# Gate, bias and token order moved to the sorted expert rows; one adding transfer a batch brings them back

## The reference

```
xn = layernorm(x)                                  # 4096 rows of 128
logits = xn @ wr + br;  top_p, top_i = top_k(softmax(logits), 2)
gate = top_p[:, 0] / (top_p[:, 0] + top_p[:, 1])   # one number a row
for e in range(8):                                 # only the rows whose first choice is e count
    hout = gelu(xn @ w1[e] + b1[e]) @ w2[e] + b2[e]
    out += where(top1 == e, hout * gate, 0)
x = x + attention(xn) @ w_proj + b_proj + out
```

## Time and profile before

| | us |
|---|---|
| median of 3 runs | 475.69 |
| the profiled execution, its own time | 475.12 |
| its span, first to last instruction | 473.5 |
| PE busy | 398.5 (84%) |
| DVE busy | 302.1 (64%) |
| ACT busy | 281.0 (59%) |
| POOL busy | 245.2 (52%) |

### The profile page before, as it was taken

The page is one execution under the profiler, slowest core; times in us unless marked ns, Lnnn a source line. Parts: engine busy times, 40 slices in busy tenths (PEclk is TensorE's granted clock), DMA queues, the critical chain, the costliest instruction groups (busy, mean ns, idle before and its releaser), DMA issues. The chain is left out here.

```text
span 473.5 us, 11202 instructions
## 1 busy us (share of the span) xinstructions
PE 398.5 (84%) x3872; PEld 233.1 (49%) x3872; DVE 302.1 (64%) x494; ACT 281.0 (59%) x692; POOL 245.2 (52%) x370
## 2 busy tenths in 40 slices
PE   3736788798989884999999899898899889899884
PEld 2435524343434342999999644344444444444322
DVE  3565389977377765255555477787778678778401
ACT  3521146466376662666666666776667657667762
POOL 6441015358568865122232358778597586653221
PEclk9775559789599997799999999999999999999987
DMA  9999013537237424122222143443354243100000
GB/s 174 259 308 276 24 47 105 154 95 228 77 115 204 130 85 107 45 71 69 66 66 66 35 94 100 142 113 97 93 141 111 81 108 80 41 9 3 24 1 24
DMA packets 45341, 48.14 MB, mean 102 GB/s; under 512 B 7393, under 2 KB 39426, under 8 KB 45170
## 3 DMA queue, kind: packets, MB, share of 16 engines
q1 hardware_dynamic: 41424, 40.41, 30.9%
q0 software_dynamic: 3296, 6.76, 4.7%
q10 hardware_dynamic: 578, 0.40, 0.3%
HBM read 25.39 MB, written 21.89 MB: 100 GB/s over the span
## 5 line engine op out<-in xcount | busy, mean ns | idle before, releaser
L570 ACT ACTIVATE probs<-ps 128x512 f32<-128x512 f32 (+2 forms) x384 | 190.6, 527 | 107.4 <-PE ps L1162 103.8
L723 DVE TENSOR_REDUCE mx<-ps 128x2 f32<-128x1024 f32 (+2 forms) x192 | 196.7, 1045 | 76.3 <-PE ps L1014 70.3
L1162 PE MATMUL ps<-stack 61*128 61x128 bf16 (+3 forms) x512 | 125.0, 313 | 21.7 <-ACT probs L570 20.4
L917 POOL TENSOR_SCALAR_AFFINE_SELECT probs<-probs 128x512 f32<-128x512 f32 x128 | 80.9, 638 | 94.0 <-ACT probs L570 91.9
L1007 PE MATMUL ps<-stack 59*128 59x256 bf16 (+3 forms) x512 | 101.2, 318 | 5.2 <-DVE mx L723 5.1
L1136 PE MATMUL ps<-probs,vt 128*18 128x512 f32 (+3 forms) x1024 | 98.0, 456 | 6.1 <-POOL probs L917 5.7
L1162 PEld LDWEIGHTS ps<-stack 61*128 61x128 bf16 x512 | 35.9, 94 | 123.3 <-ACT probs L570 82.7
L1014 PE MATMUL ps<-tri,swap_b 64*128 64x64 bf16 (+1 forms) x384 | 70.6, 206 | 0.0
L1014 PE MATMUL ps<-tri,cbf 64*128 64x64 bf16 (+1 forms) x384 | 65.2, 205 | 0.0
L899 POOL DMA_DIRECT2D ys_sorted<-yst x39 | 21.1, 540 | 62.2 <-DVE yst L775 61.9
L545 ACT ACTIVATE hid<-ps,wcur 128x128 f32<-128x128 f32 x156 | 44.8, 374 | 0.5 <-PE ps L1094 0.5
(11 more groups left out here) (119 smaller groups left out, 394.8 us busy)
## 6 DMA issues: line engine op xcount, KB each, us to landing
stack<-qk_parts SPq DMA_DIRECT2D x64, 192.0 KB, 4.3
qk_parts<-qkp SPq DMA_DIRECT2D x16, 384.0 KB, 2.6
qk_parts<-qkp SPq DMA_DIRECT2D x16, 256.0 KB, 2.5
wall<-L_ffn_w SPq DMA_DIRECT2D x16, 256.0 KB, 3.0
xs_sorted<-probs SPq DMA_DIRECT2D x1, 2496.0 KB, 11.4
xst<-xs_sorted SPq DMA_DIRECT2D x39, 64.0 KB, 1.8
ys_sorted<-yst POOLq DMA_DIRECT2D x39, 64.0 KB, 2.1
xt<-L_attn_x SPq DMA_DIRECT2D x8, 256.0 KB, 6.9
```

The lines of the kernel that those rows point to most:

```text
L570: act.activation(p[:, e, slots[0]:slots[0] + ns], ps[:, ST_BANK[c % 2], 0:ns * w].rearrange("p (s w) -> p s w", s=ns), ACT.Exp).then_inc(e ...
L723: dve.tensor_reduce(mx[:, n % 2, :, slots[0]:slots[0] + k, tb], src, AX_X, ALU.max, negate=True).then_inc(mx_done, 1)
L917: pool.affine_select(out=p, in_=p, compare_op=ALU.is_ge, fill=0.0, base=0, pattern=[[0, G], [1, P]], channel_multiplier=-1).then_inc(p_mas ...
L1162: last = pe.matmul(ps[:, ST_BANK[c % 2], i * w:(i + 1) * w], stack[at:at + N_STACK, b % 2, 1, 2 * g + s, P * sb_:P * (sb_ + 1)], stack[at: ...
```

## The change

Each normed row gets two more columns (`XW = 130` instead of 128): the gate, written there by DVE (the reciprocal of `route_gate`), and the token's number, written once by POOL at the start with an iota. Padding slots get token numbers past the real ones, by a second iota over the zeroed array. So the scatter to `xs_sorted` and the load of a sorted tile carry gate and token, in rows of 520 bytes where they had 512.

In the expert loop POOL first copies both out of the loaded tile (`tile_meta`, two copies of one column); DVE after its addition does a second operation, yst * gate + b_proj (with b_attn's part in it, `bpb`), and only that sets `ye_done`; POOL stores the tile with an indirect DMA to its tokens' places in `ys_token`. Before it takes the columns of tile n+1, POOL waits for the store of tile n-2; SP's load of a tile waits for `meta_done` beside `xsT_ps`.

After the experts, POOL issues for batch b one DMA at (n, c) = (12 + b, 4) that adds 512 rows to x in SBUF. The gathers, the multiplications by gate, the additions and the bias additions on POOL are gone.

```diff
-        xs_dram = nc.dram_tensor("xs_sorted", (NST * P, C), F32, kind="Internal").ap()
-        ys_dram = nc.dram_tensor("ys_sorted", (NST * P, C), F32, kind="Internal").ap()
+        xs_dram = nc.dram_tensor("xs_sorted", (NST * P, XW), F32, kind="Internal").ap()
+        ys_dram = nc.dram_tensor("ys_token", (NT * P + NST * P, C), F32, kind="Internal").ap()
...
             def load_tile(q, r):
                 if not first(q):
                     sp.wait_ge(xsT_ps, FR * (q - 1) + r + 1)
+                    sp.wait_ge(meta_done, FR * (q - 1) + r + 1)
...
-                dve.reciprocal(gate[:], gexp[:]).then_inc(gate_done, 1)
+                dve.reciprocal(xn[:, :, C], gexp[:]).then_inc(gate_done, 1)
...
                 dve.tensor_tensor(yst[:, r, :], ps[:, r, P:P + C], wcur[:, r, B2_AT:B2_AT + C],
-                                  ALU.add).then_inc(ye_done, 1)
+                                  ALU.add).then_inc(ye_made, 1)
+                dve.wait_ge(meta_done, FR * q + r + 1)
+                dve.wait_ge(ye_made, FR * q + r + 1)
+                dve.scalar_tensor_tensor(yst[:, r, :], yst[:, r, :], gcur[:, r:r + 1], bpb[:], ALU.mult, ALU.add
+                                         ).then_inc(ye_done, 1)
...
             pool.memset(probs[:], 0.0).then_inc(zero_made, 1)
+            pool.wait_ge(zero_made, 1)
+            pool.iota(probs[:, 0:NST * XW].rearrange("p (n w) -> p n w", w=XW)[:, :, C + 1], pattern=[[1, NST]],
+                      base=NT * P, channel_multiplier=NST, allow_small_or_imprecise_dtypes=True).then_inc(zero_made, 1)
+            pool.iota(xn[:, :, C + 1], pattern=[[P, NT]], base=0, channel_multiplier=1,
+                      allow_small_or_imprecise_dtypes=True).then_inc(tokens_made, 1)
...
+            def tile_meta(q, r):
+
+                n = FR * q + r
+                pool.wait_ge(xs_loaded[r], 16 * (q + 1))
+                pool.sem_inc(pool_passed, 1)
+                pool.tensor_copy(gcur[:, r:r + 1], xst[:, r, C:C + 1])
+                pool.tensor_copy(tok[:, r:r + 1], xst[:, r, C + 1:C + 2]).then_inc(meta_done, 1)
+
             def store_tile(q, r):
-                pool.wait_ge(ye_done, FR * q + r + 1)
+                n = FR * q + r
+                if not (final(q) and r == FR - 1):
+                    if not (first(q) and r < FR - 1):
+                        pool.wait_ge(ys_stored[(r + 1) % FR], 16 * (q if r < FR - 1 else q + 1))
+                    tile_meta(q + 1 if r == FR - 1 else q, (r + 1) % FR)
+                pool.wait_ge(meta_done, n + 1)
+                pool.wait_ge(ye_done, n + 1)
                 pool.sem_inc(pool_passed, 1)
-                pool.dma_start(ys_dram[bass.ds((FR * q + r) * P, P), :], yst[:, r, :]).then_inc(ys_stored[r], 16)
+                pool.indirect_dma_start(ys_dram, bass.IndirectOffsetOnAxis(ap=tok[:, r:r + 1], axis=0),
+                                        yst[:, r, :], None).then_inc(ys_stored[r], 16)
...
-                if n % 3 == 1 and c == 6 and n < 3 * NB:
-                    own = xt[:, TB * b:TB * (b + 1), :]
-                    pool.tensor_tensor(own, own, bpb[:].unsqueeze(1).broadcast_to([P, TB, C]), ALU.add
-                                       ).then_inc(biased, 1)
...
-                        pool.indirect_dma_start(ysg[:, d, t, :], None, ys_dram,
-                        pool.tensor_tensor(own, own, gate[:, TB * d:TB * (d + 1)].unsqueeze(2).broadcast_to([P, TB, C]),
...
+                    if (n, c) == (fold_in(d), FOLD_AT):
                         if proj_first(d):
                             pool.wait_ge(proj_added, d + 1)
-                        pool.tensor_tensor(own, own, ysg[:, d], ALU.add).then_inc(ys_added, 1)
+                        pool.dma_start(xt[:, TB * d:TB * (d + 1), :],
+                                       ys_dram[T * d:T * (d + 1), :].rearrange("(n p) c -> p n c", p=P),
+                                       accum_op=ALU.add).then_inc(folded[d], 16)
```

More of the change, by code:

```diff
@@ L26 @@
 NST = NT + E - 1
+XW = C + 2
 EPS = 1e-5
@@ L74, with fold_in @@
 LOADS, STORES = 4, 3
-FETCH_AT = (1, 5)
-def fetch_from(b):
-    return FFN_AT + 2 * b
+FOLD_AT = 4
+def fold_in(b):
+    return FFN_AT + 1 + b
 def proj_at(b):
     return NG * (b + 1) + 1
-def add_at(b):
-    return fetch_from(b) + 2 if proj_at(b) != fetch_from(b) + 2 else fetch_from(b) + 3
 def proj_first(b):
-    return proj_at(b) < add_at(b)
+    return proj_at(b) < fold_in(b)
 def block_kernel(nc, x, w_attn, b_attn, w_proj, b_proj, w1, b1, w2, b2, wr, br,
@@ L127, in block_kernel @@
         guard_p = sb("guard_p", [P, 2, P], BF16)
-        ysg = xn[:].rearrange("p (r n) c -> p r n c", n=TB)
-        xst = sb("xst", [P, FR, C])
+        xst = sb("xst", [P, FR, XW])
+        gcur = sb("gcur", [P, FR])
+        tok = sb("tok", [P, FR], U32)
         xsT = sb("xsT", [P, FR, P])
@@ L285, in block_kernel @@
         proj_added = sem("proj_added")
-        biased = sem("biased")
-        gathered = [sem(f"gathered{r}") for r in range(2)]
-        gated = sem("gated")
-        ys_added = sem("ys_added")
+        meta_done = sem("meta_done")
+        ye_made = sem("ye_made")
+        tokens_made = sem("tokens_made")
+        folded = [sem(f"folded{b}") for b in range(NB)]
         out_stored = [sem(f"out_stored{r}") for r in range(2)]
@@ L477, in normalise @@
                 act.wait_ge(nmr_done, b + 1)
-                act.activation(xn[:, t, :], xt[:, t, :], ACT.Identity, bias=nmr[:, t:t + 1], scale=rstd[:, t:t + 1]
+                act.activation(xn[:, t, 0:C], xt[:, t, :], ACT.Identity, bias=nmr[:, t:t + 1], scale=rstd[:, t:t + 1]
                                ).then_inc(xn_act_done, 1)
@@ L626, in normalise @@
                 for t in range(TB * b, TB * b + 2):
-                    last = dve.tensor_scalar(xn[:, t, :], xt[:, t, :], mv[:, t, 0:1], rstd[:, t:t + 1],
+                    last = dve.tensor_scalar(xn[:, t, 0:C], xt[:, t, :], mv[:, t, 0:1], rstd[:, t:t + 1],
                                              ALU.subtract, ALU.mult)
@@ L785, in experts @@
                 dve.wait_ge(experts_known, 1)
+                dve.wait_ge(bias_made, 1)
                 for r in range(FR):
@@ L925, in pool_at @@
                         pool.wait_ge(slots_done, 1)
+                        pool.wait_ge(gate_done, 1)
+                        pool.wait_ge(tokens_made, 1)
                         pool.wait_ge(zero_stored, 16)
@@ L969, in transposes @@
                 for t in range(TB):
-                    last = pe.transpose(ps[:, XT_BANK[b % 2], t * P:(t + 1) * P], xn[:, TB * b + t, :], ident[:])
+                    last = pe.transpose(ps[:, XT_BANK[b % 2], t * P:(t + 1) * P], xn[:, TB * b + t, 0:C], ident[:])
                 last.then_inc(xnT_ps, 1)
@@ L1084, in tile_transpose @@
                     pe.wait_ge(ye_done, n - FR + 1)
-                pe.transpose(ps[:, r, 0:P], xst[:, r, :], ident[:]).then_inc(xsT_ps, 1)
+                pe.transpose(ps[:, r, 0:P], xst[:, r, 0:C], ident[:]).then_inc(xsT_ps, 1)
             def tile_up(q, r):
```

33 lines of the change are left out of this document (8 added, 25 removed).

## The result

The kernel went from 475.23 us (474.73 to 480.38) to **488.9 us** (488.01 to 489.68, four runs each): ratio 1.025, 95% interval 1.0194 to 1.0306. The forecast was 484.0, its range 470 to 503. A later comparison of the same two kernels on another chip gave 483.55 us beside 478.28 for the kernel before, ratio 1.0073 (1.0033 to 1.0113).

A forecast was written before the change was run, and what follows sets the result against it. PE's own work was taken to bound the loop, with the wait for `ye_done` becoming the pace: 475.1 + 15.4 (loop) + 0.4 + 0.8 - 1.2 - 2.7 - 3.8 (clock) = 484.0 us, range 470 to 503.

The forecast's parts named there:

- the likeliest case: Whole kernel: the forecast itself, 484.0 us, had chance 0.60; as outcomes, slower 0.51, same 0.41, faster 0.08.
- The round over `ye_done`: Expert loop: PE's transpose of n+3 waits for DVE on n; the second operation lengthens this from 1.72 to 2.08 us.
- The collision of 0.2 us a tile: Expert loop: POOL's small copies and DVE's work disturb each other, 0.2 us a tile charged, making the tile 2.28 us.
- It holds by 0.3: Expert loop: SP's load, waiting for `meta_done`, lands in time for the transpose of n+3, with 0.3 us to spare.
- The copy round: Expert loop: the weights' copy after `ye_done` is felt by PE if delayed more than 0.1 us; no separate price.
- POOL sheds work: Outside the loop: less POOL work saves 2.7 us before it (-1 to -3.8) and 1.2 after (0 to -2.5).
- The clock of group 5: Attention, 119 to 134 us: with PE's earlier wait shortened, the half-clock stretch likely does not come, -3.8 us (0 to -4).
- The iotas: Kernel start: two iotas ahead of POOL's first normalisation, 0.2 us each, +0.4 us (0 to 0.4).
- End of the loop: After the last tile: later `ye_done`, an indirect last store and the waits behind it, +0.8 us (0.4 to 2).
- Lock: Rival, expert loop: each wide DVE copy loses 1.14 us beside POOL's indirect DMA; 2.85 us a tile, 505.7 us; chance 0.17.
- PE's pace: Rival, expert loop: the round stays at 1.85 us, below 1.9, so the loop adds 0 to 1; 469.1 us; chance 0.13.
- Rows of 520 bytes: Rival, scatter before the loop: rows cut in two make indirect DMAs a quarter longer; 493.8 us; chance 0.10.

The follow-up runs named there:

- e6: Kernel before plus a second DVE operation of the same shape on `yst` ahead of `ye_done`, POOL's work unchanged: 484.66 us, 2.071 us a tile.
- e1: Changed kernel with PE's transpose waiting for DVE's addition, not its second operation: 478.88 us, ratio 1.0035 to the kernel before, 2.121 us a tile.
- f1: Changed kernel with POOL taking gate and token of tile n+2, not n+1, ahead of the store of n, into six slots: 479.38 us, 2.116 a tile.
- e8: Changed kernel with PE's transpose waiting for DVE's addition and the weights' copy ahead of the second operation: 491.71 us, 2.387 us a tile.
- f4: Changed kernel: columns taken two tiles ahead, transpose and group 11 entry after DVE's addition, POOL's last-store wait before the first adding transfer: 474.40 us, 2.045 a tile.
- f3: As f4, with the weights' copy also ahead of DVE's second operation: 470.66 us, ratio 0.9837 to the kernel before, 1.932 us a tile.
- e3: Changed kernel plus four POOL additions of the removed bias addition's shape, on a spare tile in groups 1, 4, 7 and 10: 486.77 us, ratio 1.0154.
- e5: Changed kernel without DVE's second operation, gate and bias left out; stores, copies and adding transfers stay: 472.51 us, ratio 0.9896 to the kernel before, 1.961 a tile.
- e2: Changed kernel with POOL's wait for the last three stores moved from the loop's end to ahead of the first adding transfer: 481.0 us, ratio 1.0080.

## Why the prediction was right, and where it was not

The time was right (484.0 for 488.9, or 483.55 on the second chip) and the likeliest case was the one that came, but it came near in part by luck, since errors of size offset each other: the loop was put 4.4 us too high, and the clock behind it was left out. On the second chip the cost was 0.7%, where 1.8% was forecast.

**The round over `ye_done`: right.** e6 shows it with nothing else changed: 2.071, where I had 2.08 from dependencies alone. The parts: the second operation 352 ns, not 319; the gap between the two DVE operations 0.04 in e6, as I had, and 0.10 in the kernel after, where DVE waits for `meta_done` as well; release to PE 0.07 in the tile shown and 0.15 at the median, for my 0.14.

**The collision of 0.2 us a tile: failed.** The second operation takes at most 388 ns, 36 over its median, and the wide copy 764 at the median. The loop cost 11.0 us where this term made it 15.4; without it 38 x (2.08 - 1.875) = 7.8. What came on top, from 2.08 to 2.171, is the larger gap, the third round and the one late load. Something does collide, but POOL pays: where its one-column copies overlap the second operation they end 0.03 to 0.04 us behind it and take 0.30 to 0.35 us instead of 0.17 to 0.20 (229.49 in the timeline above). The evidence for a loss on DVE was misread: the row of 3.42 us holds three copies, and they are

```profile
L766 DVE COPY wcur<-wall x1: 762/762/762, 182.7 to 182.7; 128x1156 f32 x1
```

```profile
L766 DVE COPY wcur<-wall x1: 2002/2002/2002, 183.4 to 183.4; 128x1156 f32 x1
```

and a third of 0.75. The first lies beside the indirect DMA (182.46 to 183.54) and lost nothing; the second, which lost 1.24 us, lies beside the two masks (183.56, 1.22 us). No mask runs in the loop.

**"It holds by 0.3": failed.** I had SP's load wait for `meta_done` with 0.3 us to spare. The terms were near and the test was at the wrong place: 2.6 + 1.9 us were set against 3 T - 2.0 at T = 2.28, which had the collision in it. Without the collision, at T = 2.08, the same sum is 0.26 us short, and solved for T it gives (2.6 + 1.9 + 2.0) / 3 = 2.17 us, the step that was measured (so close by luck: the traces make it 2.15). The loads' 3.45 us of room became 0.17, and by e1, f1 and e8 the POOL round binds about as much as the bank. In the kernel after the two share the loss; f1 shows that without this round the loop would still take 2.12. The copy round I had named ("a delay of more than 0.1 us is felt too") and not priced: f4 against f3 prices it at 0.11 (0.185 over tiles 12 to 36), once the two others are gone.

**POOL sheds work: right.** Before the loop I had -2.7 and got -2.1: group 4 -0.8 (0.9), group 7 -1.2 (0.6), the stretch from group 10 to the first addition -0.5 (1.2), group 8 +0.4. After it -1.3 for -1.2: the eight adding transfers take 1.30 us each on POOL, inside the 0.54 to 2.2 allowed.

**The clock of group 5: right**, -3.8 as forecast, and e3 shows the cause: with POOL's additions back, PE's wait for POOL's mask and the fall come back together. The loop kept 1.00, as expected.

**The clock elsewhere: not in the sum.** Group 11 at 0.67 (+2.8) and the last part at 0.50 (+5.3) are 8.1 us that no term held; the second belongs to no part of the change. I had looked at what the change takes away from PE's waits and not at the place where it adds one: PE's wait for `guard_n` behind the loop was 0.44 us and became 1.12, in a stretch in which PE is busy 1.16, 1.08 and 0.66 of 2 us; and its wait for DVE behind the last tile was 0.39 and became 0.84. By e5 and e6 each of the two growths is enough.

**Small terms.** The iotas: POOL's first normalisation starts at 6.72 for 6.58, +0.1 (I had 0.4). The +1.4 up to group 3 is not theirs: e2 and f3 have them too and reach group 3 at 97.2 and 97.5 (97.3 before); in the kernel after the clock had fallen by 27 to 30 us (0.82, where before, e2 and f3 had 1.00). End of the loop +1.1 for +0.8.

**The rivals.** *Lock*: refuted, and the rows of before refuted it already (the copy of 0.76 beside the indirect DMA). In f3 the copy runs wholly beside the store, and neither waits for the other; of its timeline:

```profile
231.88 1.07 POOL L931 DMA_INDIRECT ys_token<-yst,tok  x1 [0.61 <-issue]
...
232.07 0.76 DVE L769 COPY wcur<-wall 128x1156 f32 x1 [0.24 <-DVE yst L778]
...
235.71 0.97 POOL L931 DMA_INDIRECT ys_token<-yst,tok  x1 [0.55 <-issue]
235.80 0.77 DVE L769 COPY wcur<-wall 128x1156 f32 x1 [0.24 <-DVE yst L778]
```

The Trainium skill, SBUF — State Buffer, section "Who interferes with whom", has a DVE copy in a 2-port mode and a GpSimd operation exclude each other for a whole instruction. The copy beside the masks agrees: 0.76 + 1.22 = 1.98 us, measured 2.00. For an indirect DMA it does not hold: the copy keeps 0.76 and the store pays 0.1 us (0.97 or 1.07, by where the copy falls; two of f3's 39 took 1.29 and 1.37), so there the measurement decides. *PE's pace*: refuted by 2.171, yet f3 comes near it (1.932). *Rows of 520 bytes*: refuted, the indirect DMAs of the scatter, L952 in the kernel after, for the gather of the same size before:

```profile
L952 POOL DMA_INDIRECT xs_sorted<-xn,slot x32: 958/980/1234, 102.3 to 177.2; - x32
```

## What to carry to other kernels

An operation added behind a signal lengthens every round that passes through that signal: list who waits for it, and give each waiter the earliest signal that it needs (the bank is free after the read, the weights' copy needs no gate). Rounds of nearly one length hide each other: one broken alone gains a tenth or less of what all give together (0.02 of 0.275 us a tile, tiles 12 to 36), and moving work within one can lengthen another (e8). Test each round's room at the shortest step that the other terms allow, not at one that holds a guess. A wait in a queue says only that something waited; measure the room from the landing to its use. Where work is taken from an engine that feeds TensorE, look at the clock of the next group as well as the wait; where a wait is added, do the same.

## What the hardware showed that I had not expected

- From the signal that it waits for to its start, an indirect DMA on POOL takes 0.78 to 0.80 us, in which the profile shows nothing else, beside about 1 us of its own; a plain one takes 0.73 to 0.75 (kernel before and e6). In a list of such steps that is more than POOL's two copies together (0.42).
- Two dependent DVE operations on 128 columns stand 0.04 us apart with one wait between them (e6) and 0.10 with two and another scalar (the kernel after); which of the two costs, no run shows.
- One load in a loop can land late (3.05 to 3.5 us for 1.8, once each in the kernel after, its repeat and e2). In the kernel before one landed after 2.75 us with 2.6 to spare and cost nothing; without room the late ones cost 1.2 to 1.8 us.
- A wide copy on DVE is not slowed by POOL's indirect DMA (0.76) and took 2.00 beside two of POOL's masks.
- A half-clock stretch costs 1.3 to 3.8 us in a group and up to 7 in the last four, and whether it comes there varies between executions of one program: 488.0 to 489.7 us on one chip and 478.0 to 485.1 on another for the same instructions.
- An adding transfer of 512 rows is one instruction of 1.30 us on POOL and lands 4.5 us later. It replaced four gathers of 0.97 and the arithmetic of a batch, some 7.5 us of POOL's time, and groups 12 to 27 gained 1.3 us in all, since POOL was seldom waited for there.
